# Two Gram matrices per layer from a precomputed symmetric product of the weights, in a four-layer graph network

## The reference

```
z_l = einsum('bnd,ed->bne', h, W_lang)          # 256 x 512 per batch
z_g = einsum('bnd,ed->bne', h, W_grav)
v   = einsum('bnd,ed->bne', h, W_V)
zn  = z_l / norm(z_l)
A_l = max(einsum('bnd,bmd->bnm', zn, zn), 0) * not_eye
sq  = sum(z_g * z_g)
d2  = max(sq + sq.T - 2 * einsum('bnd,bmd->bnm', z_g, z_g), 0)
A_g = exp(-d2 / (2 * sigma**2)) * not_eye
K   = w_l * row_normalised(A_l * adj) + (1 - w_l) * row_normalised(A_g * adj)
out = einsum('bne,ed->bnd', K @ v, W_O.T)
```

## Time and profile before

| | |
|---|---|
| time, median of 3 runs | 2306.62 us (2304.38 to 2306.8) |
| span of the profiled execution | 2302.1 us |
| the three executions timed, beside that span | 2304.38, 2306.8, 2306.62 us |
| PE matmul busy | 2238.5 us (97%), 15204 matmuls |
| PE weight loads busy | 2054.4 us (89%) |
| DVE busy | 1815.2 us (79%) |
| ACT busy | 814.1 us (35%) |
| POOL busy | 377.2 us (16%) |

### The profile page before, as it was taken

One profiled execution on the slowest core, in us unless ns is written; L12 is line 12 of the kernel. 1 busy time (PEld: TensorE's weight loads), 2 busy tenths in 40 slices (PEclk: granted clock), 3 DMA queues, 4 the chain that ended last, 5 costly groups with the idle time before them and its releaser, 6 DMA issues.

```text
span 2302.1 us, 39592 instructions
## 1 busy us (share of the span) xinstructions
PE 2238.5 (97%) x15204; PEld 2054.4 (89%) x15204; DVE 1815.2 (79%) x4601; ACT 814.1 (35%) x1513; POOL 377.2 (16%) x326
## 2 busy tenths in 40 slices
PE   7999999999999999999999999999999999999997
PEld 6898898989989899898988989899898998989896
DVE  7678787786878878788787877878788787887875
ACT  5424233342423424233242333424234242342421
POOL 1112021120211112011120211202111021111200
PEclk9999999999999999999999999999999999999998
DMA  5000000010000100000000000100001000000000
GB/s 183 10 1 25 15 10 29 1 38 2 10 29 2 37 1 10 29 10 29 1 23 16 10 29 1 38 2 10 29 1 38 1 11 29 10 29 1 19 1 19
DMA packets 23709, 45.45 MB, mean 20 GB/s; under 512 B 2624, under 2 KB 2880, under 8 KB 23488
## 3 DMA queue, kind: packets, MB, share of 16 engines
q1 hardware_dynamic: 23488, 42.48, 5.4%
HBM read 25.70 MB, written 16.78 MB: 18 GB/s over the span
## 4 chain that ended last, share of the span: by engine, by line
PE 82%; DVE 11%; issue 4%; ACT 1%; DMA 1%; POOL 0%; SPq 0%; DVEq 0%; POOLq 0%; ACTq 0%
PE psum L303 19%; PE psum L441 14%; PE psum L307 10%; PE psum L419 10%; PE psum L425 9%; PE psum L420 9%; PE psum L311 7%; DVE zs L809 5%; DVE full L917 2%; PE psum L375 2%; DVE stats L865 2%; PE psum L371 1%; PE psum L384 1%; ACT vs L592 1%; DVE full L1031 1%
## 5 line engine op out<-in xcount | busy, mean ns | idle before, releaser
L441 PE MATMUL psum<-zs 128*128 128x256 f32 x3072 | 398.5, 284 | 0.0
L441 PEld LDWEIGHTS psum<-zs 128*128 128x128 f32 x3072 | 382.7, 191 | 4.9
L592 ACT ACTIVATE zs<-psum 128x512 fp32r<-128x512 f32 (+1 forms) x456 | 239.3, 533 | 403.9 <-PE psum L425 314.3
L1203 POOL TENSOR_TENSOR rstd<-veps,minus_half 128x2 f32<-128x2 f32 x128 | 102.4, 800 | 1251.7 <-DVE veps L874 1251.7
L809 DVE TENSOR_TENSOR zs<-psum,zs 128x512 fp32r<-128x512 f32 (+1 forms) x456 | 266.6, 610 | 31.8 <-ACT zs L592 31.2
L592 ACT ACTIVATE vs<-psum 128x512 fp32r<-128x512 f32 x128 | 76.7, 599 | 552.0 <-PE psum L307 552.0
L311 PE MATMUL psum<-ident,full 128*128 128x128 f32 x1412 | 195.5, 278 | 48.4 <-issue 30.2
L311 PEld LDWEIGHTS psum<-ident,full 128*128 128x128 f32 x1412 | 164.8, 142 | 67.5 <-issue 38.7
L1199 POOL TENSOR_TENSOR full<-full 128x512 f32<-128x512 f32 x96 | 145.4, 1514 | 440.0 <-DVE zs L809 433.0
L865 DVE BATCH_NORM_STATS2 stats<-full 128x6 f32<-128x512 f32 x256 | 163.4, 680 | 0.0
L1031 DVE SCALAR_TENSOR_TENSOR full<-psum,rdeg,full 128x512 f32<-128x512 f32 x128 | 95.9, 749 | 82.3 <-PE psum L307 82.3
(11 more groups left out here) (139 smaller groups left out, 5104.5 us busy)
## 6 DMA issues: line engine op xcount, KB each, us to landing
full<-in_x_dram SPq DMA_DIRECT2D x32, 512.0 KB, 3.6
out_dram<-full SPq DMA_DIRECT2D x32, 512.0 KB, 2.8
full<-in_L_gnn_W_lang_dram SPq DMA_DIRECT2D x2, 1024.0 KB, 5.5
full<-in_L_gnn_W_V_dram SPq DMA_DIRECT2D x2, 1024.0 KB, 7.1
full<-in_L_gnn_W_O_dram SPq DMA_DIRECT2D x2, 1024.0 KB, 5.8
full<-in_L_gnn_W_grav_dram SPq DMA_DIRECT2D x2, 1024.0 KB, 5.5
full<-in_adj_dram SPq DMA_DIRECT2D x1, 256.0 KB, 2.6
bias_row<-in_L_gnn_bias_dram SPq DMA_DIRECT2D x1, 256.0 KB, 7.2
```

The costliest lines, as they stand in the source:

```text
L441: last = mm(psum[s][:, (3, 1)[kind], n * nodes:(n + 1) * nodes], a, b, start=(i == 0), stop=(i == 3 * FT - 1))
L592: return nc.scalar.activation(dst, src, func, **kw)
```

## The change

With S = W^T W, the Gram matrix is h S h^T. S is symmetric, so S = T + T^T, where T holds the upper triangle and half of the diagonal blocks, and the Gram matrix is G + G^T with G = h T h^T. S is formed once at the start. Per batch, layer and kind:

- `project_hi` multiplies the hi part of h by the upper blocks of T alone (10 block products, hi and lo, so 20 matmuls of 256 columns), `project_lo` multiplies the lo part by the whole of S in hi (16 matmuls); before it was 48.
- `gram` multiplies the result (hi, lo) by the hi part of h: 16 matmuls of 256 columns for 24 before.
- New: ACT copies G from PSUM to SBUF (`copy_gram`, 128x512), and PE adds its transpose onto G in PSUM with four 128x128 transposes (`symmetrise`). DVE's readers wait for `sym_done` in place of `gram_done`.
- The order of the slots is another: see the rows below. `values` is cut in `values_head` (hi*hi and hi*lo, 8 matmuls) and `values_tail` (4).
- At the start W_lang and W_grav are split in hi and lo in SBUF (`split_weight`) and multiplied by themselves (`prepare`, 48 matmuls of 512, 384, 256 and 128 columns for 16 transposes), and six blocks are mirrored below the diagonal (`mirror`). The order of loads and jobs changes with it.

```diff
-        jobs = [("l", 0), ("o", 0), ("vo", 0), ("g", 0), ("l", 1), ("o", 1), ("vo", 1), ("g", 1)]
+        jobs = [("l", 0), ("g", 0), ("o", 0), ("vo", 0), ("l", 1), ("g", 1), ("o", 1), ("vo", 1)]
...
+                        hi, lo, rest = part_hi[kind], part_lo[kind], slice(t * P, U)
+                        last = product(dst[:, rest], [(hi[:, e, cols], lo[:, e, cols], hi[:, e, rest], lo[:, e, rest])
+                                                      for e in range(FT)])
...
+            def mirror(q):
+                kind, l = jobs[q]
+                for t in range(1, FT):
+                    pe.wait_ge(prep_out, 4 * q + t + 1)
+                    for e in range(t):
+                        last = flip(psum[1][:, t, e * P:(e + 1) * P], plain(hi_of[kind, l][:, e, t * P:(t + 1) * P]))
+                    last.then_inc(mirror_pe, 1)
...
+            def project_hi(s, j, l, kind, es):
...
+                for e in es:
+                    cols = slice(e * P, (e + 1) * P)
+                    for d in range(e + 1):
...
+                        top = diag_hi(wl, d) if d == e else wh[:, d, cols]
+                        mm(project_bank(s, kind, e), top, HTH[s][:, d, :], start=(d == 0 and e % 2 == 0), stop=False)
+                        mm(project_bank(s, kind, e), wl[:, d, cols], HTH[s][:, d, :], start=False, stop=False)
...
+            def symmetrise(s, j, l, kind):
+                pe.wait_ge(gram_copied[s], j * 4 + (2 * l + kind + 1))
+                bank, half = halves(psum[s][:, (3, 1)[kind], :]), halves(M[s][:, (1, 3)[kind], :])
+                for n in range(NT):
+                    for m in range(NT):
+                        last = mm(bank[:, n, m * P:(m + 1) * P], half[:, m, n * P:(n + 1) * P], ident[:],
+                                  is_transpose=True, start=False, stop=(n == NT - 1 and m == NT - 1),
+                                  skip_group_check=True)
+                last.then_inc(sym_done[s], 1)
...
             def seam_slot(s, js, l, r, jr, jn):
...
-                gram(s, js, l, 0, 1)
+                gram(s, js, l, 1)
+                symmetrise(s, js, l, 0)
+                values_head(s, l, 0)
                 if jn is not None:
                     sum_rows(r, jn)
-                gram(s, js, l, 1, 0)
-                gram(s, js, l, 1, 1)
-                values(s, js, l, 0)
-                values(s, js, l, 1)
+                symmetrise(s, js, l, 1)
+                values_tail(s, l, 0)
+                values_head(s, l, 1)
+                values_tail(s, l, 1)
                 if jn is not None:
                     transpose_x(r, jn, 0)
...
+            def split_weight(i):
+                kind, n = parts[i]
+                act.wait_ge(w_loaded[n], 16)
...
+            def copy_gram(s, j, l, kind):
+                act.wait_ge(gram_done[s], j * 4 + (2 * l + kind + 1))
+                run(M[s][:, (1, 3)[kind], :], psum[s][:, (3, 1)[kind], :]).then_inc(gram_copied[s], 1)
...
             def squares_l(s, j, l):
-                dve.wait_ge(gram_done[s], j * 4 + (2 * l + 1))
+                dve.wait_ge(sym_done[s], j * 4 + (2 * l + 1))
```

More of the change, by code:

```diff
@@ L406, in transpose_x, with project_bank @@
                     last.then_inc(ht_done[s], 1)
-            def project(s, j, l, kind, e):
-                bank = (3, 0, 1, 2)[2 * kind + e // 2]
-                dst = psum[s][:, bank, (e % 2) * nodes:(e % 2 + 1) * nodes]
+            def project_bank(s, kind, e):
+                return psum[s][:, (3, 0, 1, 2)[2 * kind + e // 2], (e % 2) * nodes:(e % 2 + 1) * nodes]
+            def project_hi(s, j, l, kind, es):
                 wh, wl = w_hi[l]["lg"[kind]], w_lo[l]["lg"[kind]]
[L413 to L444, removed]
@@ new lines, in project_lo @@
+            def project_lo(s, j, l, kind, es):
+                wh = w_hi[l]["lg"[kind]]
+                for e in es:
+                    cols = slice(e * P, (e + 1) * P)
+                    for d in range(FT):
+                        if kind == 0 and e == 0 and d % 2 == 0:
+                            pe.wait_ge(htl_ready[s], j * 4 + (2 * l + d // 2 + 1))
+                        last = mm(project_bank(s, kind, e), wh[:, d, cols], HTL[s][:, d, :], start=False,
+                                  stop=(e % 2 == 1 and d == FT - 1))
+                last.then_inc(z_done[s], 1)
@@ new lines, in gram @@
+            def gram(s, j, l, kind):
+                pe.wait_ge(zl_ready[s], j * 8 + (4 * l + 2 * kind + 1))
+                pe.wait_ge(zh_ready[s], j * 8 + (4 * l + 2 * kind + 2))
+                bank = psum[s][:, (3, 1)[kind], :]
+                for y in (ZH[s][kind], ZL[s][kind]):
+                    for e in range(FT):
+                        if y is ZL[s][kind] and e == 2:
+                            pe.wait_ge(zl_ready[s], j * 8 + (4 * l + 2 * kind + 2))
+                        for n in range(NT):
+                            last = mm(halves(bank)[:, n, :], y[:, e, n * P:(n + 1) * P], HTH[s][:, e, :],
+                                      start=(y is ZH[s][kind] and e == 0 and n == 0),
+                                      stop=(y is ZL[s][kind] and e == FT - 1 and n == NT - 1))
+                last.then_inc(gram_done[s], 1)
@@ L1051, in start @@
                 softmax_row(0, 0)
+                split_weight(2)
+                prepare(2)
                 for t in (0, 2):
```

220 lines of the change are left out of this document (144 added, 76 removed).

## The result

The changed kernel takes 2351.0 us (median of 4; 2348.4 to 2352.8), the kernel before 2306.7 us: ratio 1.0194, 95% interval 1.018 to 1.0208. The profiled spans are 2344.8 and 2302.1 us, 42.7 us apart.

What follows compares the result with a forecast made beforehand. PE was taken to bound both slot kinds, with DVE's room 8.3 us in middle and 5.0 in seam slots. Terms -72 + 60 - 4 + 34 + 22 = +40 us on 2306.6 gave 2346, rounded to 2345; range 2285 to 2385.

Steps and rivals of the forecast that it cites:

- 32 middle slots: Middle slots: PE saves 3.95 us each, 1.7 lost waiting for normalise and norm_squares, 2.25 kept; -72 us in all.
- 30 full seam slots: Full seam slots: later sum_rows delays DVE's scaling, layer norm and normalise, 2.0 us longer each; +60 us.
- first and last seam slot: First seam slot, without kernel rows, changes by nothing; the last gains PE's 3.75 us; -4 us.
- start: Before the loop: matmuls replacing transposes, mirroring, 6.5 us in each of four jobs, plus 8 for weight splits; +34 us.
- clock in the loop: New PE gaps bring more stretches at 1.2 GHz in place of 2.4: 1.5 us more a turn, 15 turns; +22 us.
- DVE idles 2.7 us longer: Seam slot: 4.2 us of PE work between column sums and sum_rows, before 1.52, delays DVE's scaling by 2.7 us.
- It stood 0.65 us behind this: Seam slot: transpose_x on PE stood 0.65 us behind normalise, so it moves by only 2.7 - 0.65 = 2.05 us.
- I take no change: Seam slot, DVE from kernel rows to column sums, 24.1 us: no change taken, 1.4 us less or more possible.
- The first: Rival: PE stays the bound and DVE does not idle for the rows; 253 us go, 34 come, 2088 us; chance 0.10.
- The second: Rival: seam slots break even, no stretch at 1.2 GHz added; -42 us, 2265 us, half way 2285; chance 0.09.
- The third: Rival: as forecast but without further stretches at 1.2 GHz; 2324 us, inside the range, 0.2 of the forecast's chance.
- The fourth: Rival: slower still by late Gram copies (+38), more clock (+23) or a start of 42; above 2385 us; chance 0.07.

Runs made afterwards that it cites:

- experiment 1: Changed kernel with sum_rows moved directly behind gram(1), ahead of symmetrise(0) and values_head(0), in the seam slots: 2280.6 us.
- experiments 2: Changed kernel with sum_rows behind the first 8 of gram(1)'s 16 matmuls, and ACT's sum_row ahead of copy_gram(1): 2231.2 us.
- experiment 4: Kernel before the change with sum_rows moved behind gram(1) in place of ahead of it, Gram products untouched: 2406.8 us.
- Experiment 5: Changed kernel with only the middle slot reordered, mix_values and layer2 earlier on PE, ACT's and DVE's order adapted: 2302.5 us.
- experiment 6: Changed kernel with W^T W at the start formed from the hi parts alone, 16 in place of 48 matmuls a job: 2335.1 us.
- experiment 3: Changed kernel with 12 extra matmuls of 512 columns on PE in each of the 30 full seam slots, ahead of the wait for normalise: 2337.8 us.
- experiment 7: Changed kernel with sum_rows inside gram(1) in seam slots, and mix_values and layer2 early in middle slots: 2186.1 us.
- experiment 8: Kernel before the change with sum_rows earlier, behind 8 of gram(0, 1)'s 12 matmuls: 2293.8 us.

## Why the prediction was right, point by point

The forecast, 2345 us in 2285 to 2385, held: slower, by the mechanism that it named. Two of its terms were mis-sized, in opposite directions, the seam slots by some 15 us too little and the clock by 19 too much. That the sum came within 6 us of the 2351.0 measured is in part luck.

| term | predicted | measured |
|---|---|---|
| 32 middle slots | -72 | -71 (27.8 for 30.0 us) |
| 30 full seam slots | +60 | +75 (40.7 for 38.2 us) |
| first and last seam slot | -4 | about -4 |
| start | +34 | +36 (first projection at 100.34 for 64.46) |
| clock in the loop | +22 | +3 (means above the shortest turn: 1.31 for 1.07 us) |
| sum | +40 | +42.7 between the spans; 3 to 4 us are not assigned |

The seam's +75 goes by the first seam slot of a turn. By the turns without a stretch, 139.24 for 138.79 us with two middle slots of 2.2 us less, both seam slots together grew by 4.9 us, which makes it +73.

**The seam's chain.** "DVE idles 2.7 us longer": 2.77. "It stood 0.65 us behind this": that room was used up first, as foreseen, and PE waits 3.0 us where "3 us" was written. Experiments 1 and 2 show the cause, 4 shows it in the other kernel. What was too small is "2.0 us longer for each", by 0.5 us, and it lies at "I take no change" for the chain ahead of the sums. From the kernel rows to the reciprocals DVE did recover a part, 25.27 us (477.84 to 503.11) for 25.70. But it starts later. Before, the kernel rows came 1.44 us behind `norm_rows` on PE (999.93, and 1001.37 in the earlier trace rows); now 2.25, 475.59 to 477.84. The first two rows are PE's, before and after; the other three are the DVE work of the changed kernel that stands between:

```profile
999.93 0.27 PE L311 MATMUL psum<-ident,full 128*128 128x128 f32 x1
```

```profile
475.59 0.66 PE L330 MATMUL psum<-ident,full 128*128 128x128 f32 x4 [0.29 <-DVE full L1098]
```

```profile
475.45 0.68 DVE L1082 SCALAR_TENSOR_TENSOR full<-psum,adj_off 128x512 f32<-128x512 f32 x1
476.05 1.28 DVE L908 TENSOR_TENSOR xs<-psum,xs 128x512 fp32r<-128x512 f32 x2
477.24 0.68 DVE L908 TENSOR_TENSOR vs<-psum,vs 128x512 fp32r<-128x512 f32 x1
```

`norm_rows` now starts the moment DVE hands over, so the product with the mask (L1082) and the three splits (L908) that stand behind `norm_squares` on DVE are ahead of the chain instead of beside PE's work. The sum: 0.81 - 0.43 + 2.77 - 0.65 = 2.5 us. The first part is read from the traces; no run took it out alone.

**Middle slots.** "2.25 kept" is what came. PE waits 0.67 us for `normalise` and 0.3 for `norm_squares`, 32 times each; at the end of the middle slot above:

```profile
473.01 1.33 PE L330 MATMUL psum<-ident,full 128*128 128x128 f32 x8 [0.68 <-DVE full L989]
```

Experiment 5 gives back 1.5 of the 1.7 us that I had as lost.

**The start.** PE's busy time rose by 28.3 us (77.5 for 49.2) and its waiting by 7.6: 26 and 8 were taken. That they agree so closely is in part luck. The granted clock of that window is 0.95, before 1.00, so up to 5 us (0.05 x 100.3) of the rise are the clock's, for which the term had nothing; and experiment 6 got 16.6 us for the two thirds of the products that were priced at 20. It shows that they are on the path there.

**The clock.** "1.5 us more a turn" was wrong in size. The stretches at 1.2 GHz did come: 78 us of the 13 turns, for 27 us in eight stretches before. That is as if 1.2 more of them had come a turn, where about one was taken. What failed is the price. A stretch that follows the first seam slot's gap costs 0.8 us a turn and not 1.6; the slot behind it is bound by DVE (experiment 3). A window behind such a gap and one without, then the starts of three turns around them, with and without:

```profile
654.20:657.60 3.40, 3.40 (x18) 3.23 (x19) 3.26 (x7) 1.73 (x4) 0.47 (x1) 0.59 0.00 0
514.90:518.30 3.40, 3.27 (x25) 2.80 (x26) 3.40 (x7) 2.35 (x4) 0.54 (x1) 1.00 0.00 0
```

```profile
426.47 0.66 PE L330 MATMUL psum<-ident,full 128*128 128x128 f32 x4 [0.74 <-DVE full L1132]
...
565.71 0.66 PE L330 MATMUL psum<-ident,full 128*128 128x128 f32 x4 [2.07 <-DVE full L1132]
...
705.73 0.66 PE L330 MATMUL psum<-ident,full 128*128 128x128 f32 x4 [2.08 <-DVE full L1132]
```

565.71 - 426.47 = 139.24 us, 705.73 - 565.71 = 140.02. The price had been read in a kernel that PE bounds, and was used where DVE bounds. That this is the reason is argued from experiment 3, not shown by a run of its own. The Trainium skill (TensorE: Matmul & The Clock Gate, "What's actually happening") has throttling as the default that activity releases; experiment 3, which fills the waits and raises the mean clock from 0.974 to 0.990, agrees.

**The rivals.** The first, PE as the bound at 2088 us, fell with experiment 3: work added to PE cost nothing. The Trainium skill (Perfetto Trace Analysis, "Identifying the Most-Contended Engine") would have TensorE, at 89% LDWEIGHTS busy, improved first. The runs agree on where time could be had: experiment 7, with the same cut, is 120 us faster than the kernel before. But the cut did not pay by itself: with it and a longer chain through PE, ACT and DVE the kernel got slower. The second, seam slots breaking even (2265 to 2285), is close to where experiment 1 lands (2281), and took a move of `sum_rows` to be true; its "half way, 2285" should read 2295 by its own terms. The third (2324 us, no more stretches) had the clock's cost nearly right, though not for its reason, and the seam too short. The fourth did not come: PE waits for no Gram copy in the list of waits.

## What to carry to other kernels

Taking work from the bounding engine shortens the cover of every chain that leaves it and comes back, so look for each hand-over whose distance in that engine's order grows in the same edit: here four small transposes 2.8 us later cost some 2.1 us a slot, 64 in all, and moving them 3.2 us forward gave 120, about 97 of it by the chain and 11 by the clock in the loop. Price a wait by the slot's second engine and its idle time at that one instruction, not by the busy shares of the slot. And compare shortest turns as well as means, since a clock that drops after some gaps moves the total by 12 to 16 us without any slot changing (experiments 2, 3 and 8).

## What the runs showed of the hardware

- More work made the kernel faster: 360 matmuls added into waits of 2.8 to 3.0 us took 13 us off (experiment 3).
- A gap of 2.18 us was followed by a granted clock of 0.52 in one turn and 1.00 in the next; of 1.40 us by 1.00 in experiment 8, where the mean clock is 0.995. Waits of 3.02 us were followed by 1.00 in one turn and 0.59 in the next. So the gap's length alone does not decide, and what else does is open. It does weigh: at the loop's edge of the kernel before and its two variants, a stretch at 1.2 GHz stood at 1 of 14 gaps of 1.40 to 1.86 us (experiment 8), at 8 of 14 of 1.86 to 2.39 us (before), and at all 14 of 2.77 to 3.35 us (experiment 4).
- The loop's edge does not show as "issue" on PE after the change, but the time is there. DVE has 30.0 us of "issue" in 14 places, and `transpose_k`, in the slot behind the edge alone, waits 0.6 to 2.3 us for DVE. With such a wait (2.07 us, at 565.71) the middle slot that follows the edge takes 30.05 us (556.99 to 587.04), before 30.08 plus the gap of 2.18.
- Four fp32 transposes issued with `start=False` onto a filled bank take 0.35 us (504.93 to 505.28), as four that overwrite one (1028.41 to 1028.76 in the earlier trace rows).
